# Causal attention with DMA-queue transposes of the normalised input and of the heads' result, and the gating's steps moved to where the output's stood

## What is computed

```python
def _dense_bf16(x, W, b):
    return jnp.matmul(x.astype(jnp.bfloat16), W.astype(jnp.bfloat16)) + b.astype(jnp.bfloat16)
def _attention(q, k, v, mask):            # 16 heads of 16 features
    scores = jnp.einsum('bhqd,bhkd->bhqk', q, k) * scale
    full_mask = causal[None, None] & (mask[:, None, None, :] > 0)
    p = jax.nn.softmax(jnp.where(full_mask, scores, -jnp.inf), axis=-1)
    return jnp.einsum('bhqk,bhkd->bhqd', p, v)
```

## Time and profile before

| what | value |
|---|---|
| median of 3 runs | 1894.02 us (1893.44 to 1898.48) |
| the profiled execution's own time | 1898.35 us |
| its span (first to last instruction) | 1896.4 us |
| PE / DVE / ACT / POOL busy, whole span | 89% / 62% / 59% / 38% |
| mean granted TensorE clock | 0.966 of full speed |
| attention stage, turn 0 to the last logits | about 82 to 446 us of the span |

### The profile page before, as it was taken

The page is one execution under the profiler, slowest core; times in us unless marked ns, Lnnn a source line. Parts: engine busy times, 40 slices in busy tenths (PEclk is TensorE's granted clock), DMA queues, the critical chain, the costliest instruction groups (busy, mean ns, idle before and its releaser), DMA issues. The chain is left out here.

```text
span 1896.4 us, 40651 instructions
## 1 busy us (share of the span) xinstructions
PE 1680.2 (89%) x13348; PEld 1385.9 (73%) x13348; DVE 1182.2 (62%) x4060; ACT 1121.5 (59%) x2587; POOL 722.1 (38%) x886
## 2 busy tenths in 40 slices
PE   6777778787999999999997899999999899999995
PEld 5555555565788888888996777777777677777774
DVE  6798888876301101101113899999995788888884
ACT  5598888882222222222334666666564788888884
POOL 4434444431211111100104466656654244545544
PEclk9899999987999999999998999999999899999997
DMA  3101110104955555655975200000000200111110
GB/s 131 49 3 43 30 30 30 30 27 147 314 173 182 200 171 179 202 167 169 335 256 168 71 23 19 15 23 23 23 28 1 76 28 26 35 35 36 35 63 29
DMA packets 111695, 171.95 MB, mean 91 GB/s; under 512 B 6832, under 2 KB 86576, under 8 KB 110864
## 3 DMA queue, kind: packets, MB, share of 16 engines
q1 hardware_dynamic: 95248, 142.55, 22.8%
q0 software_dynamic: 6480, 17.70, 3.1%
q10 hardware_dynamic: 9776, 9.31, 1.4%
HBM read 143.45 MB, written 26.08 MB: 89 GB/s over the span
## 5 line engine op out<-in xcount | busy, mean ns | idle before, releaser
L2191 ACT ACTIVATE moe_hT<-moe_p_h,lane_a 128x256 f32<-128x256 f32 (+1 forms) x344 | 131.6, 434 | 370.1 <-PE moe_p_h L2146 370.1
L2146 PE MATMUL moe_p_h<-moe_gT,moe_w 128*128 128x256 f32 (+1 forms) x1376 | 255.7, 344 | 0.8 <-issue 0.8
L2156 PE MATMUL moe_p_y<-moe_w,moe_hT 128*128 128x256 f32 x1136 | 252.3, 379 | 0.0
L2146 PEld LDWEIGHTS moe_p_h<-moe_gT,moe_w 128*128 128x128 f32 x1376 | 227.2, 191 | 25.5 <-issue 1.0
L2074 POOL DMA_INDIRECT moe_gx<-moe_tokens,moe_source_i x71 | 67.5, 951 | 458.2 <-PE moe_p_t L2133 401.2
L1731 ACT ACTIVATE xb_pr<-xb_sc,xb_nmax 128x256 f32<-128x256 f32 x512 | 222.8, 503 | 30.2 <-DVE xb_nmax L1814 28.5
L2156 PEld LDWEIGHTS moe_p_y<-moe_w,moe_hT 128*128 128x128 f32 x1136 | 212.5, 190 | 27.1
L1112 ACT ACTIVATE xa_pr<-xa_sc,xa_nmax 128x256 f32<-128x256 f32 (+1 forms) x512 | 203.7, 452 | 35.1 <-DVE xa_nmax L1211 34.7
L1814 DVE CUSTOM_DVE_ANT_0 xb_sc<-xb_p_s,begun_area 128x256 f32<-128x256 f32 x512 | 187.1, 419 | 41.7 <-PE xb_p_s L1562 39.1
L2283 DVE COPY moe_gT<-moe_p_t 128x512 f32<-128x512 f32 (+1 forms) x43 | 25.7, 599 | 233.1 <-PE moe_p_t L2133 226.1
L2308 DVE TENSOR_TENSOR moe_gy<-moe_p_y,lane_a 128x256 f32<-128x256 f32 x71 | 27.5, 421 | 229.0 <-PE moe_p_y L2156 229.0
(11 more groups left out here) (374 smaller groups left out, 3459.6 us busy)
## 6 DMA issues: line engine op xcount, KB each, us to landing
moe_w<-in_L_ffn_w_dram SPq DMA_DIRECT2D x86, 1024.0 KB
begun_area<-xb_kv SPq DMA_DIRECT2D x32, 256.0 KB, 2.9
moe_rows_out<-moe_gy ACTq DMA_DIRECT2D x28, 256.0 KB
xb_kv<-moe_w SPq DMA_DIRECT2D x18, 256.0 KB, 3.0
X<-in_x_dram SPq DMA_DIRECT2D x4, 1024.0 KB, 9.6
xa_ctx<-in_ctx_turned_dram SPq DMA_DIRECT2D x16, 256.0 KB, 3.1
moe_tokens<-moe_XN SPq DMA_DIRECT2D x16, 256.0 KB, 2.2
xb_raw<-in_fside_BxSxS_dram SPq DMA_DIRECT2D x15, 256.0 KB, 3.7
```

The lines of the kernel that those rows point to most:

```text
L2146: last = pe.matmul(p_h[n % 3][:, k * width:(k + 1) * width], w1[:, r, ic, (2 * n + k) * P:(2 * n + k + 1) * P], gT[:, r % 2, ic, 0:width], ...
L2156: last = pe.matmul(p_y[:, t * D:(t + 1) * D], hT[:, hc, t * P:(t + 1) * P], w2[:, r, hc, :], start=(hc == 0), stop=(hc == HC - 1))
L2191: last = act.activation(hT[:, 2 * n + k, 0:width], p_h[n % 3][:, k * width:(k + 1) * width], ACT.Gelu, bias=b1[:, bass.ds(e * HC + 2 * n + ...
```

## The change

Four edits, all in `causal_attention`:

1. PE's transposes of the normalised input and of the heads' result (four each in a turn) and ACT's two reads of them are gone. SP issues four DMA transposes a turn in their place: two of 128x256 for the input (`turn_x`), two for the heads' result (`turn_outputs`). They stand in SP's list behind `load(b+1)`.
2. The input is measured and normalised two turns ahead and no longer one. Its `norm` moves on DVE from step 1 to step 2.
3. The gate's transposes and logits move to the place in step 0 where the output stood, one turn later than before (b-4). The output's projection, read and bias move to step 2.
4. `measure_gate(b-2)` moves on DVE from the end of step 2 to the end of step 3, the last thing of the turn. On POOL, `finish_values` now stands ahead of `gate_root` and `gate_norm`.

```diff
@@ SP
+            def turn_x(n):
+                sp.wait_ge(s_["normed"], n)
+                if n >= 2:
+                    sp.wait_ge(s_["q_proj"], n - 1)
+                for t in range(TB):
+                    sp.dma_start(xT[:, :, t * P:(t + 1) * P], xn[:, t, :], transpose=True).then_inc(xT_in, 16)
+
+            def turn_outputs(n):
+                if n >= 1:
+                    sp.wait_ge(s_["y_ready"], n)
+                for t in range(TB):
+                    sp.wait_ge(s_["o_ready"], TB * n + t + 1)
+                    sp.dma_start(oT[:, :, t * P:(t + 1) * P], o[:, t, :], transpose=True).then_inc(oT_in, 16)
 
             for b, h, s in turns(sp):
...
                     load(b + 1, h + s, 1 - s)
+                if b == 0:
+                    turn_x(1)
+                if has_next(b, 2):
+                    turn_x(b + 2)
+                if b >= 1:
+                    turn_outputs(b - 1)
+            turn_outputs(B - 1)
@@ POOL
-                    root(b + 1)
+                if b == 0:
+                    root(1)
+                if has_next(b, 2):
+                    root(b + 2)
                 if since(b, 2):
                     add(b - 2)
+                if has_next(b):
+                    finish_values(b + 1, 1 - s)
+                if since(b, 2):
                     gate_root(b - 2)
                     if b - 2 < B - 1:
                         gate_norm(b - 2)
-                if has_next(b):
-                    finish_values(b + 1, 1 - s)
@@ PE
             def project_queries(n):
-                pe.wait_ge(s_["x_ready"], n)
+                pe.wait_ge(xT_in, 16 * TB * n)
                 project(0, xT, s_["q_proj"])
+
+            def project_outputs(n):
+                pe.wait_ge(oT_in, 16 * TB * (n + 1))
+                project_rows(oT, 3, s_["y_ready"])
...
                     if g == 1 and has_next(b):
-                        if b >= 3:
-                            pe.wait_ge(s_["m_x_ready"], b - 2)
-                        elif b >= 1:
+                        if b >= 1:
                             pe.wait_ge(s_["o_ready"], TB * (b - 1) + 1)
                         project_keys(b + 1)
@@ DVE
-                    if g == 0 and has_next(b):
-                        measure(b + 1)
-                    if g == 0 and since(b, 2):
-                        bias_output(b - 2)
-                    if g == 1 and has_next(b):
-                        norm(b + 1)
+                    if g == 0:
+                        if at(b, 0):
+                            measure(1)
+                        elif has_next(b, 2):
+                            measure(b + 2)
...
+                    if g == 2 and b >= 1 and has_next(b, 2):
+                        norm(b + 2)
...
+                    if g == 2 and since(b, 2):
+                        bias_output(b - 2)
                     if g == 2 and has_next(b):
                         finish_queries(b + 1, 1 - s)
-                    if g == 2 and b >= 2:
+                    if g == 3 and b >= 2:
                         measure_gate(b - 2)
```

More of the change, by code:

```diff
@@ L877, in _ @@
         def _(pe):
[L878 to L883, removed]
             def project(n, src, done):
@@ L990, in _ @@
                         scores(b, s, g)
-                    if g == 0 and since(b, 2):
+                    if g == 0 and b >= 4:
                         if runs(b):
                             pe.wait_ge(s_["v_read"], b)
[L994 to L1002, removed]
+                        else:
+                            pe.wait_ge(s_["o_ready"], TB * (b - 1))
+                        turn_gate(b - 4)
+                    if g == 2 and since(b, 2):
+                        if has_next(b):
+                            pe.wait_ge(s_["k_read"], b + 1)
+                        else:
+                            pe.wait_ge(s_["o_ready"], TB * (b - 1) + 1)
+                        project_outputs(b - 2)
                     if g == 3 and since(b, 1):
@@ L1022, in _ @@
                     if g == 2 and has_next(b):
[L1023 to L1024 removed]
+                        if b >= 2:
+                            pe.wait_ge(s_["y_read"], b - 1)
+                        else:
+                            pe.wait_ge(s_["k_read"], b + 1)
                         project_queries(b + 1)
@@ L1142, in _ @@
                         exponentials(b, STEP * g)
-                    if g == 1 and b >= 3:
-                        read_gate(b - 3)
+                    if g == 0 and b >= 4:
+                        read_gate(b - 4)
+                    if g == 2 and since(b, 2):
+                        read_projected(b - 2)
                     if m is not None:
@@ L1148, in _ @@
                         exponentials(b, STEP * g + 1)
-                    if g == 0 and since(b, 2):
-                        read_projected(b - 2)
+                    if g == 0 and b >= 4:
+                        read_logits(b - 4)
+                    if at(b, B + 1):
+                        read_projected(B - 1)
                     if g == 1 and has_next(b):
@@ L1269, in _ @@
                         shift_unit(b, s, STEP * g + 3)
-                    if g == 0 and has_next(b):
-                        measure(b + 1)
-                    if g == 0 and since(b, 2):
-                        bias_output(b - 2)
-                    if g == 1 and has_next(b):
-                        norm(b + 1)
+                    if g == 0:
[3 more added lines that the diff above has]
+                            measure(b + 2)
+                    if g == 2 and at(b, 0):
+                        measure(2)
+                    if at(b, B + 1):
+                        bias_output(B - 1)
+                    if g == 2 and b >= 1 and has_next(b, 2):
+                        norm(b + 2)
+                    if g == 1 and at(b, 0):
+                        norm(1)
+                    if g == 3 and at(b, 0):
+                        norm(2)
                     if m is not None:
```

51 lines of the change are left out of this document (16 added, 35 removed).

## The result

The changed kernel takes 1931.44 us, median of 5 runs (1928.42 to 1933.83), beside 1894.02 (1891.36 to 1898.48) for the kernel before: ratio 1.0196, 95% interval 1.0177 to 1.0214. It is slower by 37.4 us, where 26 were forecast. The profiled execution took 1932.73 us with a span of 1929.4.

A forecast was written before the change was run, and what follows sets the result against it. Hand-overs between DVE and ACT, both 88% busy, were taken to bound the kernel. Turn 0 +2, turns 1-2 -1, turns 3-14 +23, turn 15 -0.5, tail +3 make +26.5 us: 1920 us forecast, 8-in-10 range 1897 to 1937.

The forecast's parts named there:

- The cause: Attention turns: measuring the gate at the turn's end makes measurement, norm, store, context load, cast and keys a loop; +23 us.
- The loop: Turns 3 to 14: gate measurement round through POOL, SP, PE and DVE to the next; 23.7 us a turn against 21.76.
- measurement to normalised tokens: From the end of DVE's gate measurement to the end of POOL's norm of the tokens: 4.15 us.
- normalised tokens to cast: From the end of POOL's norm, through SP's store and context load, to POOL's cast: 3.86 us.
- keys to scores, clock included: PE from key projection to next scores: 1.99 us at full clock, 2.8 with the average clock loss.
- DVE, shift to the end of the measurement: DVE's steps 2 and 3, from the first shift of the scores to the gate measurement's end: 11.5 us.
- The clock: PE's clock falls behind its wait of at least 2 us ahead of the keys, losing 0.8 us an average turn.
- The turns ahead of the loop: Turn 0 costs +2 us, queries waiting for bare transposes; turns 1 and 2 give -1 in all.
- the rival in which the loop binds barely: Clock stays up, landing short: 22.2 us a turn, +5 us in all, 1899 us or less; chance 0.10.
- The transposes: SP's DMA transposes, taken at 3.2 us each, cost nothing in the turns and are bare only at the ends.
- the bound of 8.3: Time in us from the last transpose's issue to the context load; each us over it costs a us a turn.
- The signs named: Profile after: keys wait about 2 us for `xa_cT`, store about 4.2 us after measurement, DVE's idle time moves ahead of step 2.

The follow-up runs named there:

- load-first run: Changed kernel with SP issuing the next batch's context load ahead of the store of the tokens, not behind it; 1905.83 us, ratio 1.0059 to the kernel before.

## Why the prediction was right, and where it was off

**The cause held.** The load-first run is the test: two calls swapped, and the 12 turns fall from 24.11 us to 21.95. Of the rest of the theory, that the measurement's place alone decides, the runs took a part away: its old place opens the loop and gains next to nothing, for DVE's way to the second normalisation is then the limit.

**The loop, forecast 23.7 us, is 24.2 from store to store.** By its terms, read in the turn above and in the mean of the 12 turns:

| term | forecast | this turn | mean |
|---|---|---|---|
| measurement to normalised tokens | 4.15 | 4.15 (289.85 to 294.00) | 4.18 |
| normalised tokens to cast | 3.86 | 3.38 (269.71 to 273.09) | 3.72 |
| cast to keys | 0.7 | 0.76 | 0.76 |
| keys to scores, clock included | 2.8 | 3.16 (273.85 to 277.01) | 2.81 |
| scores to shift | 0.66 | 0.87 | 0.79 |
| DVE, shift to the end of the measurement | 11.5 | 11.97 (277.88 to 289.85) | 11.94 |

The sums are 24.29 in this turn and 24.2 in the mean. The mis-sized term is DVE's: I took the queries' widening at its row of before, and it stands beside POOL's add now, 0.8 us longer. Without it DVE's part would have been 11.2.

**The clock.** The loss of 0.8 us for an average turn came out: the mean from keys to scores is 2.81 us, for 1.99 at the full clock. The turn shown lost more, 1.17, since its products at 275.14 took 1.94 us behind the wait. In three of the 12 turns the way took 1.97 us and nothing was lost, behind waits of 2.73, 2.01 and 1.80 us; in the other nine it took 2.56 to 3.66. So a wait of this length goes with a lower clock often, not always.

**The turns ahead of the loop** were the worst estimate for their size. Turn 0 got 2.3 us longer (forecast 2), since the queries wait for the transposes (PE). The load of turn 1 stands in SP's list behind the transposes of item 2, and its cast waits for it (POOL):

```profile
96.49 1.01 PE L908 MATMUL xa_p_a<-xa_xT,lane_b 128*128 128x256 bf16 x4 [2.29 <-DMA xa_xT<-xa_xn]
```

```profile
110.36 0.61 POOL L810 CAST xa_cT<-xa_ctx 128x512 bf16<-128x512 f32 x1 [1.26 <-DMA xa_ctx<-in_ctx_turned_dram]
```

The queries start at 96.49 us, and 96.5 was forecast, but that is luck: two errors cancel. I took 0.4 us for the second issue and 3.2 for the landing; one issue takes 1.2 us and the landing 2.4. Turns 1 and 2 were to give 1 us back and took 1.2 more. The forecast had overlooked the load behind the transposes; turn 1 is as long as before nevertheless, and turn 2 is 1.25 us longer. That lies in its step 3 (8.12 us for 6.75): the wait for the second normalisation is 2.84 us for 2.43, the granted clock 0.79 for 1.00, and the measurement now ends the step. Which of these weighs most was not tested.

**The sum.** By the first scores of the turns: +3.4 up to turn 3 (forecast +1), +27.1 in the 12 turns (+23), +3.1 from turn 15 to the last logits (+2.5). The total is 33.5 us to the last logits, and 33.0 in the span. The two profiled executions differ by 34.4 us and the medians by 37.4; the rest is the spread between executions. One sum of the prediction leaves a term out: the rival in which the loop binds barely has +5 us for the turns but not the +3.5 of the ends, and so lay near 1903 and not at 1899.

**The transposes** cost nothing in the turns, as forecast: one transfer of 128x256 lands 2.3 to 2.4 us (median) after its issue, under the 3.2 taken and far under the bound of 8.3. The estimate of 2.6 us from the Trainium skill, page "VectorE: DVE Perf Modes", section "The three transpose paths", is near that. On the rule of the Trainium skill, page "Advanced Engine Details and Errata", section "X-Bar Transpose (TRN2)", that they are as fast as ordinary DMAs, no run here decides: a transpose of 64 KB takes about as long to land as the store of 256 KB (2.2 us, median) and less than the load of 256 KB (2.9), but no ordinary transfer of 64 KB is there to set beside it.

**The signs named** came out: keys wait for `xa_cT`, 2.3 us; the store 4.18 us behind the measurement; DVE's idle time moved to step 2. POOL's wait for the context was forecast near 2 us and is 3.5. The path to the cast is no longer for that, since `finish_values` now stands ahead of the gate's normalisation and POOL comes to the cast sooner.

## What to carry to other kernels

When a step moves later in a loop, follow what it releases over every queue, also through calls that merely stand behind one another there: here a store and an unrelated load in one queue tied the end of a turn to the middle of the next, and swapping the two was worth 26 us. Here it was opened at the queue, and moving the work back gained next to nothing. Look for the limit right behind the loop first, since a step put "early" may stand ahead of what another engine waits for. Where a short wait of PE stands ahead of much of its work, its price can be that of the clock behind it as well: here 2.5 us in a turn for 0.9 us of wait.

## What the runs showed of the hardware

- Two turns with 217 instructions on PE and 101 on DVE each took 23.99 and 21.46 us, at a granted clock of 0.87 and 0.92. The first has a wait of PE of 1.38 us, the second, in the run with the gate's copy first, one of 0.46 us. The same wait of 1.38 us also stands in a turn at a clock of 1.00, and of two waits of 2.06 us in one run the clock fell behind one.
- A DMA transpose of a 128x256 bf16 tile holds SP for 1.17 us (heads' result) and 1.24 us (input) in the median at its issue, three times the 0.37 to 0.42 of the store and the load beside it. It lands 2.3 to 2.4 us after its issue.
- Two bf16 operations on DVE took 1.40 us beside POOL's add and 0.62 without it; the first of them took 1.14 us for 0.35.
- The count of packets on the page of the profile rose from 111695 to 129550 with 62 transposes, and that of packets under 512 B from 6832 to 24688, which is 288 of these for each transpose. With 26 transposes more, in the run with the input transposed twice, the time stayed the same.
